# In the last pair of heads, ScalarE copies both halves of a weighted sum and GpSimd adds them

## The reference, cut to what matters

```
xn = group_norm(x)
q, k, v = split(W_qkv @ xn + b)
weight = softmax(scale * q^T k, axis=keys)
a = weight @ v
out = x + W_proj @ a + b_proj
```

## Time and profile before

| | us |
|---|---|
| median of 3 runs | 4324.97 (4324.69 to 4325.98) |
| the profiled execution | 4325.91 |
| its span | 4323.8 |
| TensorE busy | 4282.4 (99%) |
| VectorE busy | 3287.5 (76%) |
| ScalarE busy | 2918.6 (67%) |
| GpSimd busy | 2435.6 (56%) |

### The profile page before, as it was taken

How to read it: one execution, slowest core, us unless ns; L and a number is a source line. 1 busy time by engine, 2 the same in 40 slices (tenths; PEclk the granted TensorE clock), 3 DMA queues, 4 the chain that set the end, 5 groups by cost and what they waited for, 6 DMA issues and landing times.

```text
span 4323.8 us, 89926 instructions
## 1 busy us (share of the span) xinstructions
PE 4282.4 (99%) x26692; PEld 3739.6 (86%) x26692; DVE 3287.5 (76%) x5479; ACT 2918.6 (67%) x5375; POOL 2435.6 (56%) x2332
## 2 busy tenths in 40 slices
PE   8999999999999999999999999999999999999999
PEld 6888888888888888888888888888888888888888
DVE  5777867788686886877867778687886877868787
ACT  4757847577575775757757577575775757767576
POOL 5655556465564655646566465564655646556464
PEclk9999999999999999999999999999999999999999
DMA  3232222322223222232222222222222222222222
GB/s 87 49 96 47 71 72 49 96 47 78 65 49 96 47 80 65 47 95 49 78 74 58 87 47 82 64 65 80 47 79 67 66 79 48 80 64 68 75 49 88
DMA packets 99645, 295.08 MB, mean 68 GB/s; under 512 B 15104, under 2 KB 15232, under 8 KB 99328
## 3 DMA queue, kind: packets, MB, share of 16 engines
q1 hardware_dynamic: 99328, 291.19, 25.0%
HBM read 123.36 MB, written 33.55 MB: 36 GB/s over the span
## 4 chain that ended last, share of the span: by engine, by line
PE 94%; DVE 3%; POOL 2%; issue 1%; ACT 1%; DMA 0%; DVEq 0%; SPq 0%; POOLq 0%
PE ps_t L780 21%; PE ps_g L734 15%; PE ps_o L792 11%; PE ps_o L793 11%; PE ps_s L771 11%; PE ps_s L769 11%; PE ps_s L734 7%; PE ps_t L734 4%; PE ps_o L734 2%; POOL x_raw L382 2%; DVE xn_lo L644 1%; DVE rstd_bits L630 0%; DVE seed L628 0%; ACT xn_hi L491 0%; DVE pt_lo L587 0%
## 5 line engine op out<-in xcount | busy, mean ns | idle before, releaser
L376 POOL TENSOR_SCALAR probs<-probs,row_rcp 128x1024 f32<-128x1024 f32 x1024 | 1154.2, 1127 | 1365.8 <-DVE row_rcp L582 1365.8
L578 DVE TENSOR_REDUCE row_min<-ps_s 128x1 f32<-128x1024 f32 x1024 | 1250.6, 1221 | 213.4 <-PE ps_s L771 198.6
L480 ACT CAST pt_hi<-ps_t 128x512 fp32r<-128x512 f32 x2048 | 1112.6, 590 | 432.2 <-PE ps_t L780 421.7
L587 DVE TENSOR_TENSOR pt_lo<-ps_t,pt_hi 128x512 fp32r<-128x512 f32 x2048 | 1309.5, 680 | 9.5 <-ACT pt_hi L480 5.0
L475 ACT ACTIVATE probs<-ps_s,row_min 128x1024 f32<-128x1024 f32 x1024 | 1150.9, 1124 | 211.0 <-DVE row_min L578 194.2
L780 PEld LDWEIGHTS ps_t<-const_sb,probs 128*128 128x128 f32 x8192 | 945.1, 140 | 180.1 <-DVE pt_lo L587 50.3
L780 PE MATMUL ps_t<-const_sb,probs 128*128 128x128 f32 x8192 | 1084.4, 274 | 3.6 <-DVE pt_lo L587 3.4
L792 PE MATMUL ps_o<-pt_hi,v_st 128*128 128x256 f32 x4096 | 1044.1, 288 | 0.0
L793 PE MATMUL ps_o<-pt_lo,v_st 128*128 128x256 f32 x4096 | 1015.0, 282 | 0.0
L771 PE MATMUL ps_s<-kl_st,q_st 128*128 128x512 f32 x2048 | 808.5, 395 | 0.0
L769 PE MATMUL ps_s<-kh_st,q_st 128*128 128x512 f32 x2048 | 806.9, 394 | 0.0
(11 more groups left out here) (117 smaller groups left out, 4959.8 us busy)
## 6 DMA issues: line engine op xcount, KB each, us to landing
wqk_raw<-in_wqk SPq DMA_DIRECT2D x130, 256.0 KB, 2.6
q_st<-kh_st SPq DMA_DIRECT2D x128, 256.0 KB, 2.9
q_st<-kl_st SPq DMA_DIRECT2D x128, 256.0 KB, 3.6
kh_st<-kh_st SPq DMA_DIRECT2D x128, 256.0 KB, 2.9
kl_st<-kl_st SPq DMA_DIRECT2D x128, 256.0 KB, 3.6
x_raw<-layer_out SPq DMA_DIRECT2D x36, 512.0 KB, 5.4
wv_raw<-in_wv SPq DMA_DIRECT2D x66, 256.0 KB, 4.4
x_raw<-in_x SPq DMA_DIRECT2D x32, 512.0 KB, 5.5
```

The source lines that it names most:

```text
L376: nc.gpsimd.tensor_scalar(probs[m % 2][:, :], probs[m % 2][:, :], row_rcp[:, m % 4:m % 4 + 1], 1.0, ALU.mult, ALU.mult).then_inc(probs_rea ...
L480: nc.scalar.copy(pt_hi[:, m // 2 % 2, 4 * half:4 * half + 4, (m % 2) * P:(m % 2 + 1) * P], ps_t[:, half, :].rearrange("p (b t) -> p b t", ...
L578: nc.vector.tensor_reduce(row_min[:, m % 4:m % 4 + 1], ps_s[:, m % 2, :], AX.X, ALU.min).then_inc(min_ready, 1)
L587: nc.vector.tensor_tensor(pt_lo[place], ps_t[:, half, :].rearrange("p (b t) -> p b t", b=4), f32(pt_hi[place]), ALU.subtract).then_inc(lo_ ...
```

## The change

In the last pair of each pass:

- ScalarE's `other_half` becomes `both_halves`: a copy of the half on the near partitions to a new buffer `o_same`, then the copy to `o_part` as before. It also waits for the sum k-2 (the buffers' last reader).
- VectorE's `add_halves` is gone. GpSimd's `sum_halves` adds `o_same` and `o_part` into `attn`: for k = 0 to 5 in the steps 2k+4, ahead of the scaling of tile m+2, and for k = 6 and 7 between the last splits. It first waits for its own scaling before, and afterwards for its own addition.
- TensorE's `weigh` waits for the copies (`part_ready`) in place of the addition.

The other three pairs keep one copy and VectorE's addition.

```diff
@@ -93,6 +93,7 @@
         v_st = [sb(f"v_st{s}", [P, BLK, 2 * D], F32R) for s in range(2)]
         attn = sb("attn", [P, T], F32)
         o_part = [sb(f"o_part{s}", [P, GROUP], F32) for s in range(2)]
+        o_same = [sb(f"o_same{s}", [P, GROUP], F32) for s in range(2)]
         a_hi = sb("a_hi", [P, PAIRS, T], F32R)
         a_lo = sb("a_lo", [P, PAIRS, T], F32R)
         probs = [sb(f"probs{s}", [P, T], F32) for s in range(2)]
@@ -394,6 +395,17 @@
                 split_wv(0, k)
             split_wqk(1, 1, 0)
 
+            def sum_halves(pair, k):
+
+                rows = slice(0, D) if k < 4 else slice(D, P)
+                cols = slice((k % 4) * GROUP, (k % 4 + 1) * GROUP)
+                pool.wait_ge(part_ready, 8 * pair + k + 1)
+                if k < 4:
+                    pool.wait_ge(a_ready, a_at(pair - 1, k))
+                nc.gpsimd.tensor_tensor(attn[rows, cols], o_same[k % 2][rows, :], o_part[k % 2][rows, :],
+                                        ALU.add).then_inc(attn_ready, 1)
+                pool.wait_ge(attn_ready, sum_at(8 * pair + k))
+
             def attn_split(pair, p, k):
                 cols = slice(k * GROUP, (k + 1) * GROUP)
                 src = attn[:, cols].rearrange("p (o t) -> p o t", o=1)
@@ -410,6 +422,9 @@
                     hd = H * i + hh
                     for j in range(NT):
                         m = NT * e + j
+                        if last and m >= 4 and m % 2 == 0:
+                            pool.wait_ge(probs_ready, tile + m + 2)
+                            sum_halves(pair, m // 2 - 2)
                         if j == 1 and not (last and e == 1):
                             split_qk(hd + 1, 1 - e, 1)
                         if j == 3 and not (last and e == 1):
@@ -423,7 +438,13 @@
                             split_qk(hd + 2, e, 0)
                         if not (last and m + 2 >= PT_STEPS):
                             normalise(tile + m + 2, m + 2)
+                if last:
+                    pool.wait_ge(a_ready, a_at(pair, 1))
+                    sum_halves(pair, 6)
                 attn_split(pair, p, 2)
+                if last:
+                    pool.wait_ge(a_ready, a_at(pair, 2))
+                    sum_halves(pair, 7)
                 attn_split(pair, p, 3)
                 if last:
                     with pool.If(i < PASSES - 1):
@@ -480,6 +501,14 @@
                 nc.scalar.copy(pt_hi[:, m // 2 % 2, 4 * half:4 * half + 4, (m % 2) * P:(m % 2 + 1) * P],
                                ps_t[:, half, :].rearrange("p (b t) -> p b t", b=4)).then_inc(hi_ready, 1)
 
+            def both_halves(g, k):
+
+                src, dst = (slice(D, P), slice(0, D)) if k < 4 else (slice(0, D), slice(D, P))
+                act.wait_ge(attn_ready, sum_at(g - 2))
+                act.wait_ge(pv_done, pv_at(g))
+                nc.scalar.copy(o_same[k % 2][dst, :], ps_o[dst, 0:GROUP])
+                nc.scalar.copy(o_part[k % 2][dst, :], ps_o[src, 0:GROUP]).then_inc(part_ready, 1)
+
             def other_half(g, k):
 
                 src, dst = (slice(D, P), slice(0, D)) if k < 4 else (slice(0, D), slice(D, P))
@@ -531,8 +560,10 @@
                         high_part(tile + m, m, 0)
                         high_part(tile + m, m, 1)
 
-                        if m == PT_STEPS - 1 or last and m >= 3 and m % 2 == 1:
-                            other_half(8 * pair + (m - 3) // 2, (m - 3) // 2)
+                        if last and m >= 3 and m % 2 == 1:
+                            both_halves(8 * pair + (m - 3) // 2, (m - 3) // 2)
+                        elif m == PT_STEPS - 1:
+                            other_half(8 * pair + 6, 6)
                         if not (last and m + 2 >= PT_STEPS):
                             exponential(tile + m + 2, m + 2, 2 * (tile + m) + 2)
                         if j in (3, 7) and not last:
@@ -542,7 +573,10 @@
                         if e == 1 and j in (4, 6):
                             attn_high(pair, p, (j - 4) // 2)
                 attn_high(pair, p, 2)
-                other_half(8 * pair + 7, 7)
+                if last:
+                    both_halves(8 * pair + 7, 7)
+                else:
+                    other_half(8 * pair + 7, 7)
                 attn_high(pair, p, 3)
                 if last:
                     with act.If(i < PASSES - 1):
@@ -690,8 +724,8 @@
                         smallest(tile + m + 2, m + 2)
                     low_part(tile + m, m, 0)
                     low_part(tile + m, m, 1)
-                    if m == PT_STEPS - 1 or last and m >= 3 and m % 2 == 1:
-                        add_halves(pair, (m - 3) // 2)
+                    if not last and m == PT_STEPS - 1:
+                        add_halves(pair, 6)
                     if not (last and m + 2 >= PT_STEPS):
                         reciprocal(tile + m + 2, m + 2)
                     if last and m == PT_STEPS - 2:
@@ -702,7 +736,8 @@
                         channel_stats(i + 1, c - 1)
                     channel_stats(i + 1, KT - 1)
                     group_spread(i + 1)
-                add_halves(pair, 7)
+                else:
+                    add_halves(pair, 7)
 
             with dve.Fori(0, PASSES) as i:
                 lay = i // B
@@ -781,10 +816,14 @@
                                                  probs[m % 2][:, (4 * half + b) * P:(4 * half + b + 1) * P], ident)
                     mm.then_inc(transposed, 1)
 
-            def weigh(tile, g, hd, k, lo, hi):
+            def weigh(tile, g, hd, k, lo, hi, last=False):
 
                 if lo == 0:
-                    pe.wait_ge(attn_ready, sum_at(g - 1))
+
+                    if last and k > 0:
+                        pe.wait_ge(part_ready, g)
+                    else:
+                        pe.wait_ge(attn_ready, sum_at(g - 1))
                     pe.wait_ge(v_ready, hd + 1)
                     pe.wait_ge(lo_ready, lo_at(tile + 2 * k + 1, 1))
                 for b in range(lo, hi):
@@ -852,7 +891,7 @@
                             later_qk(i, m, hd, e, j)
                         if m >= 2:
                             k = (m - 2) // 2
-                            weigh(tile, 8 * pair + k, H * i + 2 * p + k // 4, k, 4 * (m % 2), 4 * (m % 2) + 4)
+                            weigh(tile, 8 * pair + k, H * i + 2 * p + k // 4, k, 4 * (m % 2), 4 * (m % 2) + 4, last)
                         if not last and m == PT_STEPS - 1:
                             later_qk(i, m, hd, e, j)
 
@@ -897,7 +936,7 @@
                 project(0, 6, 9)
                 for q in (1, 2):
                     project(q, 0, 9)
-                weigh(TILES * i + PT_STEPS * (PAIRS - 1), GROUPS * (i + 1) - 1, H * i + H - 1, 7, 0, BLK)
+                weigh(TILES * i + PT_STEPS * (PAIRS - 1), GROUPS * (i + 1) - 1, H * i + H - 1, 7, 0, BLK, True)
                 wait_alone(pe, lo_ready, lo_at(TILES * (i + 1) - 1, 1))
                 average_means(i + 1)
                 project(3, 0, 9)
```

## The result

The changed kernel takes 4371.3 us (median of 4 runs, 4369.77 to 4371.75), the kernel before 4324.83 us (4 runs, 4323.85 to 4325.98). The ratio is 1.0107, 95% interval [1.0089, 1.0124]: 46.5 us or 1.07% slower. Forecast were 4362.4 us, 37.4 us more, and a range of 4339 to 4372.

A forecast was written before the change was run, and what follows sets the result against it. It took a ring of ScalarE, VectorE and TensorE, 5.85 us per two steps, as the bound. Six loops in 16 passes at 0.39 us add 37.4 us, all else nothing: 4362.4 us, range 4339 to 4372.

The forecast's parts named there:

- The loop: Ring of ScalarE, VectorE and TensorE over two steps of the last pair: 5.85 us before, near 6.24 us after.
- VectorE's lost addition brings nothing: VectorE, last pair: the 0.41 us addition is hidden behind the wait for ScalarE's exponential, so removing it gains nothing.
- Rival 1: VectorE's queue is the bound and losing the addition frees it: 10.4 us faster in all, 4314.6 us; chance 0.06.
- The price of the copy, 0.39 us: ScalarE's second copy, between weighted sum and exponential, overlaps neither neighbour and adds 0.39 us to each loop.
- Rival 2: ScalarE's 0.36 us of idle time ahead of its copy takes the second copy; time stays at 4325 us; chance 0.08.
- Rival 3: ScalarE's two copies overlap, the second starting 0.27 us after the first: 25.9 us more, 4350.9 us; chance 0.20.
- How often, six times a pass: Copies for k = 0 to 5 delay transposes in each of 16 passes: 6 x 16 x 0.39 = 37.4 us.
- GpSimd gets the addition ... I cost it at nothing: GpSimd's 0.74 us addition, 0.94 us with waits, fits into 1.47 us idle between odd and even tiles' scalings: no cost.
- Its own sign for a loss elsewhere: In the profile after, TensorE waiting for probs or for part_ready would put the loss elsewhere than the loop.
- Rival 4: GpSimd's late addition makes a_hi at step 12 hold ScalarE, 0.5 us a pass: 8 us more, 4370 us; chance 0.10.
- the bounds of the copy: ScalarE's second copy costs at least 0.15 and at most 0.42 us per loop: 4339 to 4365 us.
- the block of k = 7: End of the last pair: block ready near 1356.2 us, TensorE asks for it at 1357.58, so no cost.

## Why the prediction was right, and where it was not

- **The bound.** The loop was read rightly. 6.24 us was forecast for it and 6.23 is measured, in the changed kernel and with the copy alone.
- **VectorE's lost addition brings nothing.** Right. The loop is 5.85 us without the addition and without the copy, as it is with VectorE's addition. Rival 1 is refuted by that run. Only at step 13 was the addition not quite hidden: with the copy alone it is 3.12 us from the transposes of step 12 to those of step 13, and 3.02 once the addition is gone, some 1.5 us in 16 passes. VectorE's idle time ahead of the reciprocal was forecast near 0.8 us and is 1.12, because most of the loop's growth falls into it as well; the forecast left that out.
- **The price of the copy, 0.39 us.** Measured 0.38, and 36.5 us by itself where the sum had 37.4. Rival 2 is refuted by the same run. Rival 3, an overlap of 0.10 us, does not hold for this pair of copies, but does for two copies of the same partitions (0.27 us, third copy). The Trainium skill ("ScalarE: Activation LUTs", section "What ACT_TABLE_LOAD costs") gives an overlap of 93 ns for ACTIVATEs that follow one another, without a condition on their partitions. The trace agrees with it for copies of the same partitions (0.37 - 0.27 = 0.10 us) and not for a copy that changes them (none), and there the measurement decides.
- **How often, six times a pass.** Right for the copy by itself: 96 times 0.38 us is the measured 36.5. In the changed kernel the loop with step 4 has the stall at step 6 in place of it, so there a further copy counts on five loops, as the third copy shows.
- **"GpSimd gets the addition ... I cost it at nothing".** This step failed. The 1.47 us of cover was read between the scalings of tiles 9 and 10 and taken for all such pairs. At step 4 the weight split stands in GpSimd's queue, there is no idle time before the scaling of tile 6 (1316.91, no bracket), and the addition was placed ahead of the split. Price: 7.4 us by the run that moves it. In the arrangement without a second copy the whole loss is 12.0 us. The prediction does not name this split, which stands in the kernel between the place of the addition and the scaling of tile 6. Its own sign for a loss elsewhere, TensorE waiting for probs, is what the profile shows.
- **Rival 4, a late GpSimd,** had the right engine and the wrong place. At step 12 a_hi came without a wait. At step 14 it waited 1.4 us for the sum of k=5, and as forecast nothing came of it. The range reached up to 4372 only for this rival; with the bounds of the copy it ended at 4365. So that 4371.3 lies inside is luck: two losses that the prediction had put at nothing, at step 4 and behind step 15, brought the time 8.9 us above the forecast, near the 8 us that it allowed for another one.
- **The rest, behind step 15.** 36.5 + 7.4 = 43.9 of 46.5 us. From the transposes of step 15 to the first transposes of the next pass it is, as a mean of the 15 such stretches of a trace, 59.63 us before and the same with the copy alone, 59.86 in the changed kernel, 59.88 with the sum of k=0 moved back and 60.08 with the third copy. So 3.5 us of the loss lie here. The prediction put the block of k = 7 at nothing, because TensorE asks for it late enough. That is so, but there is VectorE beside it, with the group norm of the next pass. In the kernel before:

```profile
1355.81 0.17 DVE L627 TENSOR_SCALAR neg_half<-var_eps 128x4 f32<-128x4 f32 x1
1355.86 2.54 POOL L349 TENSOR_TENSOR pt_lo<-wv_raw,pt_hi 128x512 fp32r<-128x512 f32 x2
```

and in the changed one:

```profile
1369.01 0.32 DVE L661 TENSOR_SCALAR neg_half<-var_eps 128x4 f32<-128x4 f32 x1
1369.26 2.54 POOL L350 TENSOR_TENSOR pt_lo<-wv_raw,pt_hi 128x512 fp32r<-128x512 f32 x2
```

In this pass GpSimd begins a_lo of k = 7, the instruction ahead of this pt_lo, 10.71 us after step 15's transposes began in the kernel before, 10.93 in the changed one and 11.19 with the third copy. VectorE's neg_half begins 11.36 to 11.37 us after them in all three, but lasts 0.17, 0.32 and 0.58 us; in the latter two it ends 0.07 us after GpSimd has gone on to pt_lo. What follows it, up to the normalisation of the next image, begins at 16.98, 17.20 and 17.44 us. So the later a_lo makes VectorE's small instruction longer, and TensorE waits at the start of the next pass. This is read from the timelines, not tested.
- **All together.** From the transposes of step 0 to those of step 15 of the last pair, summed over the 16 passes of the traces, the copy alone adds 35.9 us, the addition's leaving VectorE takes away 1.5, and the sum of k=0 ahead of the split adds 8.8. With the 3.5 us behind step 15 that is 46.7 us, for 46.5 measured.

## What to carry to other kernels

Before an instruction is put into a queue with idle time, follow that queue through every iteration that gets it, not one typical iteration: the one that holds a rare long piece of work has no cover. Two costs on one loop need not add up either: where TensorE is already held for another reason, the copy cost nothing. Where engines wait for one another in a ring, the place of a small copy in its queue counts for more than its engine: ahead of the exponential two copies cost 46.5 us, behind it nothing. An addition taken off an engine is no gain as long as that engine still waits behind it for the same event, but it can free an order of work that was not to be had before, as here the copies behind the exponential.

## What the runs showed of the hardware

ScalarE's instructions overlapped with the next by 0.10 us, so that two copies of 64x256 that last 0.37 us each start 0.27 us apart. Around a copy from the partitions 64 to 127 to 0 to 63 they start 0.38 to 0.40 us apart, and so they do where a copy on 64 to 127 is followed by an exponential on all. The change of the first partition is the one reading that fits every pair looked at here. It was not tested by itself.

Idle time stood on both sides of GpSimd's addition at step 4, where it waits for its own last instruction: 0.37 us ahead of it and 0.29 us behind it. Ahead of the additions of k = 1 to 3 it was 0.16 us, and ahead of that of k=0 in the run that moves it 0.27. The additions of k = 4 and 5, which have that wait too but not the one for `a_ready`, start 0.08 to 0.09 us after the end of the scaling. What the wait for its own instruction costs by itself was not separated from this.

VectorE's `neg_half`, 128x4, lasts 0.17 us in the kernel before. It lasts 0.32 and 0.58 us where GpSimd's a_lo, 128x256 from SBUF, is still under way beside it, and then ends 0.07 us after GpSimd's next instruction has begun.
